# The receiver's linear term folded into the update's weights, and a table of normalised and raw rows for the edge gathers

## The reference, cut to what matters

```python
h = relu(layernorm(x))
m = concat([h[dst], h[src]]) @ W_pre.T + b_pre           # one message per edge
mx, mn, mean, std = segment max, min, mean, std of m over dst (0 for no edge; std = sqrt(relu(var) + 1e-5))
agg = concat([mx, mn, mean, std]);  log_deg = log(max(deg, 1) + 1)
out = concat([h, agg, agg*log_deg, agg/log_deg]) @ W_post.T + b_post
x = x + out @ W_lin.T + b_lin
h = relu(layernorm(x))
s = segment mean of edge_attr over dst
x = x + relu(concat([h, s]) @ W1 + b1) @ W2 + b2
```

## Time and profile before

| | |
|---|---|
| median of 3 runs | 1868.22 us (1868.07 to 1869.76) |
| profiled execution, span from first to last instruction | 1776.9 us |
| what lies around the span (difference of the two) | 91.3 us |
| busy in the span: PE / DVE / ACT / POOL | 86 / 89 / 60 / 73 % |
| HBM read and written | 98.3 MB and 38.8 MB |
| node pass, about | 40 to 540 us of the span |
| edge pass, about | 541 to 1777 us |

### The profile page before, as it was taken

How to read it: one execution, slowest core, us unless ns; L and a number is a source line. 1 busy time by engine, 2 the same in 40 slices (tenths; PEclk the granted TensorE clock), 3 DMA queues, 4 the chain that set the end, 5 groups by cost and what they waited for, 6 DMA issues and landing times.

```text
span 1776.9 us, 34948 instructions
## 1 busy us (share of the span) xinstructions
PE 1526.8 (86%) x8869; PEld 1275.2 (72%) x8869; DVE 1572.7 (89%) x5261; ACT 1067.4 (60%) x2368; POOL 1302.7 (73%) x1379
## 2 busy tenths in 40 slices
PE   2899999999997788888787879878787878888895
PEld 2799898998996577767675767667676667676774
DVE  5999999999996899989798979989797979899992
ACT  1899999999996455545454545545454545455541
POOL 1778777787787878877677777867786877778643
PEclk8899999999998899999999999989998999989997
DMA  2233333233325222222122221222122222222200
GB/s 75 83 101 106 95 105 104 97 106 99 102 95 142 61 68 69 69 63 63 54 71 70 70 68 52 73 70 73 48 73 71 75 70 69 66 60 75 70 18 17
DMA packets 104065, 134.10 MB, mean 75 GB/s; under 512 B 17344, under 2 KB 63577, under 8 KB 103978
## 3 DMA queue, kind: packets, MB, share of 16 engines
q1 hardware_dynamic: 85162, 98.55, 19.1%
q0 software_dynamic: 18816, 34.71, 6.7%
HBM read 98.27 MB, written 38.79 MB: 77 GB/s over the span
## 4 chain that ended last, share of the span: by engine, by line
DVE 42%; PE 36%; issue 17%; ACT 2%; POOL 1%; DMA 1%; DVEq 1%; SPq 0%; POOLq 0%; ACTq 0%
PE bank L556 10%; PE bank L565 5%; DVE runs L1204 3%; DVE runs L1189 3%; DVE part L1083 3%; DVE var L1240 3%; DVE var L1234 3%; DVE runs L1193 2%; PE bank L577 2%; PE bank L575 2%; DVE runs L1161 2%; PE bank L539 2%; PE bank L576 2%; DVE bn L1262 2%; PE bank L547 2%
## 5 line engine op out<-in xcount | busy, mean ns | idle before, releaser
L598 PE MATMUL bank<-comb_lo,agg_hi 128*128 128x384 f32 x588 | 221.7, 377 | 44.6 <-DVE nx L1092 36.5
L473 POOL DMA_INDIRECT y<-nout,oidx x196 | 212.2, 1083 | 54.6 <-issue 51.9
L460 POOL DMA_INDIRECT xs<-in_x,idx x196 | 203.1, 1036 | 65.0 <-issue 63.7
L460 POOL DMA_INDIRECT xd<-in_x,idx x196 | 185.5, 947 | 59.7 <-issue 59.4
L602 PE MATMUL bank<-comb_hi,agg_lo 128*128 128x384 f32 x588 | 209.6, 357 | 4.0 <-POOL agg_lo L400 4.0
L599 PE MATMUL bank<-comb_hi,agg_hi 128*128 128x384 f32 x588 | 209.0, 355 | 0.0
L556 PE MATMUL bank<-w_sb,nut 128*128 128x128 f32 x1568 | 203.8, 284 | 5.4 <-DVE nout L999 4.7
L377 POOL TENSOR_TENSOR runs<-nx,b_all 128x512 f32<-128x512 f32 x98 | 125.7, 1283 | 108.6 <-DVE nx L1009 107.6
L556 PEld LDWEIGHTS bank<-w_sb,nut 128*128 128x128 f32 x1568 | 185.6, 194 | 23.1 <-issue 14.2
L400 POOL TENSOR_TENSOR agg_lo<-whole,agg_hi 128x512 fp32r<-128x512 f32 x98 | 146.1, 1513 | 66.1 <-ACT agg_hi L848 66.1
L605 PE MATMUL bank<-comb_sd,agg_sd 128*128 128x384 f32 x392 | 169.9, 517 | 0.0
(11 more groups left out here) (196 smaller groups left out, 4788.3 us busy)
## 6 DMA issues: line engine op xcount, KB each, us to landing
xs<-in_x SPq DMA_DIRECT2D x98, 256.0 KB, 2.8
y<-nout SPq DMA_DIRECT2D x98, 256.0 KB, 2.8
inv<-inv_row SPq DMA_DIRECT2D x49, 256.0 KB, 4.6
attr<-in_edge_attr SPq DMA_DIRECT2D x48, 256.0 KB
keep<-keep_row SPq DMA_DIRECT2D x49, 128.0 KB, 2.7
reset<-reset_row SPq DMA_DIRECT2D x49, 128.0 KB, 3.1
lift<-lift_row SPq DMA_DIRECT2D x49, 128.0 KB, 4.0
xs<-in_x,idx POOLq DMA_INDIRECT x196
```

The costliest lines, as they stand in the source:

```text
L460: pool.indirect_dma_start(out=rows[:, s, j, :], out_offset=None, in_=x, in_offset=bass.IndirectOffsetOnAxis(ap=idx[:, s, which, j:j + 1], ...
L473: pool.indirect_dma_start(out=out, out_offset=bass.IndirectOffsetOnAxis(ap=oidx[:, c % 4, j:j + 1], axis=0), in_=eout[:, c % 2, j, :], in_ ...
L598: pe.matmul(acc[:, 0:SCALERS * P], hi, w_lo, start=(a == MX), stop=False, skip_group_check=True)
```

## The change

1. a is no longer computed. The aggregates are taken of b + b_pre, and a's share of max, min and mean goes into the weights of h[dst]: `comb_h` (three scalers, 384 wide) = Wd times the sums of the `comb` blocks of max, min and mean, plus `comb_x` for the first scaler. It is computed once at the start (9 + 4 more products on PE). This drops a's three matmuls and the three `whole` sums, and makes the last three products of each `layer0` 384 wide instead of 128. For nodes without an edge `comb_x` stays.
2. ACT copies b + b_pre from bank 3 to bank 4 (new, `e_b`), and the scans read bank 4; the square takes the bias too.
3. The node pass writes a table in HBM: for each node 256 floats, the normalised row (before the relu) and the raw row. The edges gather the normalised half for senders (512 B) and both halves for receivers (1 KB, one descriptor per row as before), so the edge pass has no first layernorm: eight statistics, eight aggregations and two small operations less on DVE, one square root and eight activations less on ACT.
4. The gathers wait until the whole table is stored. PE's transposes wait for the gathers directly.
5. The x rows of a node chunk now land with a row pitch of 1 KB in SBUF (512 B pieces), the load comes one step later (k+5) and waits for the table store of the chunk that had the slot.

```diff
+    table = nc.dram_tensor("table", [N, 2 * P], F32, kind="Internal").ap()
+    table_halves = table.rearrange("n (t f) -> (n t) f", t=2)
+    rows = sb("rows", [P, 4, TILES, 2 * P])
+    nh, nx = rows[:, :, :, 0:P], rows[:, :, :, P:2 * P]
+    hd, xd = nh, nx
...            SP, node_step
-                c = k + 6
+                c = k + 5
                 if node(c):
                     if c >= 4:
-                        sp.wait_ge(sem("n_norm1"), c - 3 + NU * i)
-                        sp.wait_ge(sem("n_norm1_act"), c - 3 + NU * i)
-                        sp.wait_ge(sem("n_norm1_pool"), c - 3 + NU * i)
+                        sp.wait_ge(sem(f"n_tabled{c % 4}"), 16 * (c // 4) + 16 * i)
+                        sp.wait_ge(sem("n_turn1"), c - 3 + NU * i)
                         sp.wait_ge(sem("n_xc"), c - 3 + NU * i)
                     sp.dma_start(nx[:, c % 4], node_rows(x, c, i)).then_inc(sem(f"n_in{c % 4}"), 16)
+                c = k + 2
+                if node(c):
+                    sp.wait_ge(sem("n_norm1"), c + 1 + NU * i)
+                    sp.wait_ge(sem("n_norm1_act"), c + 1 + NU * i)
+                    sp.wait_ge(sem("n_norm1_pool"), c + 1 + NU * i)
...
+                    sp.dma_start(node_rows(table, c, i), rows[:, c % 4]).then_inc(sem(f"n_tabled{c % 4}"), 16)
...            POOL, edge_step
                     if c == 0:
                         pool.wait_ge(sem("turned_out"), TURNS)
-                        pool.wait_ge(sem("n_norm1"), NODE_CHUNKS)
-                        pool.wait_ge(sem("n_norm1_act"), NODE_CHUNKS)
+                        for n in range(4):
+                            pool.wait_ge(sem(f"n_tabled{n}"), 16 * ((NODE_CHUNKS - n + 3) // 4))
+                        pool.wait_ge(sem("n_turn1"), NODE_CHUNKS)
...
-                        pool.wait_ge(sem("e_norm1"), c - 3 + EU * i)
-                        pool.wait_ge(sem("e_norm1d"), c - 3 + EU * i)
+                        pool.wait_ge(sem("e_turned_s"), c - 3 + EU * i)
+                        pool.wait_ge(sem("e_turned_d"), c - 3 + EU * i)
...
-                        for which, rows in ((0, xs), (1, xd)):
+                        for which, to, of in ((0, hs, table_halves), (1, rows, table)):
...            PE
+            for s in range(SCALERS):
+                for a in (MX, MN, ME):
+                    b = 1 + s * AGGS + a
+                    pe.matmul(bank[5][:, (1 + s) * P:(2 + s) * P], w_post_sb[:, b * P:(b + 1) * P], w_lin_t[:],
+                              start=(a == MX), stop=(a == ME))
...
-                for h, w in ((hdt, comb_x_lo), (hdl, comb_x_hi), (hdt, comb_x_hi)):
-                    mm = pe.matmul(acc[:, 0:P], h[:, c % 2, cols], w[:], start=False, stop=(w is comb_x_hi and h is hdt),
+                for h, w in ((hdt, comb_h_lo), (hdl, comb_h_hi), (hdt, comb_h_hi)):
+                    mm = pe.matmul(acc[:, 0:SCALERS * P], h[:, c % 2, cols], w[:].rearrange("p s f -> p (s f)"),
...            PE, edge_step
-                    pe.wait_ge(sem("e_norm1"), c + 1 + EU * i)
+                    pe.wait_ge(sem(f"e_gathered{c % 4}"), 16 * 2 * TILES * (c // 4 + 1) + 16 * 2 * TILES * i)
...
-                    pe.matmul(bank[4][:], wd_lo[:], hdt[:, c % 2, :], start=True, stop=False)
-                    pe.matmul(bank[4][:], wd_hi[:], hdt[:, c % 2, :], start=False, stop=False)
-                    pe.wait_ge(sem("e_hdl"), c + 1 + EU * i)
-                    pe.matmul(bank[4][:], wd_hi[:], hdl[:, c % 2, :], start=False, stop=True).then_inc(sem("e_a_psum"), 1)
...            ACT
+                    act.activation(bank[4][:], bank[3][:], ACT.Identity, bias=b_pre_col[:]).then_inc(sem("e_b"), 1)
...
-                    norm1(hs, xs, 0, sem("e_norm1"))
...
-                    norm1(hd, xd, TILES, sem("e_norm1d"))
...            DVE (the scans read bank 4; L1125, L1134, L1149, L1170, L1175 and L1253 go as well)
-                    dve.scalar_tensor_tensor(whole[:, MX, :], bank[4][:], b_pre_col[:], run_max[:, b, :],
-                                             ALU.add, ALU.add).then_inc(sem(f"e_whole{MX}"), 1)
```

More of the change, by code:

```diff
@@ L519, in _ @@
             mm.then_inc(sem("turned"), 1)
+            pe.wait_ge(sem("part_sum_ready"), 1)
+            for s in range(SCALERS):
+                to = bank[5][:, s * P:(s + 1) * P]
+                mm = pe.matmul(to, w_pre_sb[:, 0:P], part_sum[:, s, :], start=True, stop=(s > 0))
+                if s == 0:
+                    mm = pe.matmul(to, w_post_sb[:, 0:P], w_lin_t[:], start=False, stop=True)
+            mm.then_inc(sem("comb_h_psum"), 1)
             pe.wait_ge(sem("comb_copied"), 1)
@@ L538, in node_step @@
                     for j in range(TILES):
[L539 removed]
+                        mm = pe.transpose(bank[0][:, j * P:(j + 1) * P], nh[:, c % 4, j, :], ident[:])
                     mm.then_inc(sem("n_turn1"), 1)
@@ L812, in edge_step @@
                     act.wait_ge(sem("e_b_psum"), c + 1 + EU * i)
+                    if c >= 1:
+                        act.wait_ge(sem("e_sum"), c + EU * i)
+                    act.activation(bank[4][:], bank[3][:], ACT.Identity, bias=b_pre_col[:]).then_inc(sem("e_b"), 1)
                     if c >= 2:
                         act.wait_ge(sem("e_sqsum"), c - 1 + EU * i)
[L815 to L833 removed]
+                    act.activation(bsq[:, c % 2, :], bank[3][:], ACT.Square, bias=b_pre_col[:]).then_inc(sem("e_bsq"), 1)
                 c = k - 1
@@ L839, in edge_step, with high_part @@
                     act.activation(h2t[:, c % 2, :], bank[0][:], ACT.Relu).then_inc(sem("e_h2t"), 1)
-                if edge(k + 2):
-                    norm1(hd, xd, TILES, sem("e_norm1d"))
-                def high_part(a, rows):
+                def high_part(a, made, rows):
                     c = k + 1
-                    act.wait_ge(sem(f"e_whole{a}"), c + 1 + EU * i)
+                    act.wait_ge(sem(made), c + 1 + EU * i)
                     if c >= 2:
@@ L1120, in edge_step @@
                     dve.reciprocal(rs2[:, b, :], sd2[:, b, :]).then_inc(sem("e_rs2"), 1)
-                if edge(k + 2):
-                    b, s = k % 2, (k + 2) % 4
-                    for j in range(2):
-                        dve.bn_stats(bn1[:, b, TILES + j, :], xd[:, s, j, :])
                 if behind:
@@ L1130, in edge_step @@
                                              ALU.mult, ALU.mult).then_inc(sem("e_ms2"), 1)
-                if edge(k + 2):
-                    b, s = k % 2, (k + 2) % 4
-                    for j in range(2, TILES):
-                        last = dve.bn_stats(bn1[:, b, TILES + j, :], xd[:, s, j, :])
-                    last.then_inc(sem("e_bn1"), 1)
-                    dve.wait_ge(sem("e_bn1"), k + 3 + EU * i)
                 if ahead:
@@ L1143, in edge_step @@
                                              ALU.max, ALU.subtract).then_inc(sem("e_hdl"), 1)
-                elif edge(k + 2):
-                    dve.memset(stats_go[:], 0.0)
-                if edge(k + 2):
-                    b = k % 2
-                    for j in range(2 * TILES):
-                        last = dve.bn_aggr(mv1[:, b, j, :], bn1[:, b, j, :])
-                    last.then_inc(sem("e_mv1"), 1)
                 if have:
@@ L1247, in edge_step @@
                     mix_plain(k, 2, i)
-                if edge(k + 3):
-                    c, b, s = k + 3, (k + 3) % 2, (k + 3) % 4
-                    dve.wait_ge(sem(f"e_gathered{s}"), 16 * 2 * TILES * (c // 4 + 1) + 16 * 2 * TILES * i)
-                    for j in range(TILES):
-                        dve.bn_stats(bn1[:, b, j, :], xs[:, s, j, :])
                 if have:
```

154 lines of the change are left out of this document (49 added, 105 removed).

## The result

The kernel after took 1674.6 us (median of four, 1669.5 to 1676.5) beside 1868.7 us of before (four, 1868.1 to 1869.8): a ratio of 0.896, 95% interval 0.894 to 0.897. The forecast was 1777 in a range of 1748 to 1842.

A forecast was written before the change was run, and what follows sets the result against it. DVE was taken to bound the edge pass before, POOL after at 22.2 us a step: first gather 549.1, 82 to k=2, 43 steps 954.6, tail 100, span 1686, plus 91.3 around it, 1777 us, range 1748 to 1842.

The forecast's parts named there:

- With the 91.3 around it: Last line of the sum: 91.3 us outside the profiled span, added to a span of 1686 to give 1777 us.
- Setup: Before the node pass: additional PE products for the new weights delay everything after by 4.4 us, bounds +2 and +7.
- The table's store: Node pass: storing 512 KB per chunk takes 3.6 us, 2.0 fixed plus 1.6, with room enough on DMA.
- (b): Node pass: held by its slots as latencies rise; 1816 us at a store plus load of 13 us; chance 0.10.
- POOL's own step, 22.17 us: Edge pass: POOL's step without its wait, 23.29 - 1.12 us; the change removes nothing from it.
- rival (e): Edge pass: POOL gets faster if its operations miss DVE, steps of 21.5 us, -30, 1747 us; chance 0.08.
- The round's stall: Edge loop: DVE's 7.1 us stand once per round stays or shrinks, covered by about 11 us of slack; may vanish.
- Rival (a): Edge loop: DVE's stand once per round is exposed, wholly or in part, up to +61, 1795 to 1838 us; chance 0.11.
- (c): Edge pass: 1 KB rows cost two descriptors, up to 1.02 us more per receiver gather, +200, 1977 us; chance 0.07.
- (d): Edge pass: PE becomes the bound as its clock falls below 0.89; at 0.85 +47, 1824 us; chance 0.06.
- (f): Edge pass: no gain because a chain over several engines holds the step at 23 to 24 us, 1830 to 1870; chance 0.02.
- DVE is the bound: Edge pass of before: DVE, 88% busy, sets the pace, since PE and POOL wait for it; POOL has almost no slack.

## Why the prediction was wrong where it was, and right where it was

**"With the 91.3 around it"** was the step that failed, in the last line of the sum. I took the difference between the profiled span and the timed median for a cost outside the program, which both kernels would pay. It was inside the program: the timed executions ran a slower edge pass than the profiled one, by the trace of a second execution 81 us in the 43 steps and 9.5 in the stand at 566 us, less 3 elsewhere. The runs beside the result put 194 us on the change; in a session where before ran quick it was worth 109. My forecast of the gain, 91 us, was a sum for the quicker rhythm, and is 18 us off there.

**The span, 18 us too long**, term by term: first gather at 544.39, forecast 549.1 (-4.7). From there to k=2 83.4, forecast 82 (+1.4). The 43 steps 944.0, forecast 954.6 (-10.6). From there to the end 95.9, forecast 100 (-4.1).

**Setup** (+4.4 forecast) and hand-over (+3.2): the first gather was at 541.54 in before, so they cost 2.9 us together and not 7.6. The L379 ahead of the first gather starts at 540.68, where the old L377 started at 539.69: the setup costs 1.0. PE made the additional products, but began with them at 21.02 instead of 23.34, which the sum had not looked for. The other 1.9 are the hand-over, with 1.5 us in which POOL waits for the last table store. **The table's store** lands in 2.7 us, the page says:
```profile
table<-rows SPq DMA_DIRECT2D x98, 512.0 KB, 2.7
rows<-in_x SPq DMA_DIRECT2D x98, 256.0 KB, 3.1
```
I had 3.6 by doubling a transfer's share, and the Trainium skill's formula (DMA: Bandwidth & Descriptors, Anatomy of one DMA) gives 3.2; that section is about DMAs that GpSimd issues, and this one is issued by SyncE. Both are too high: twice the bytes cost nothing beside the 2.8 us of 256 KB. Node steps kept their pace, so (b) did not happen, as argued.

**POOL is the bound afterwards**: right, and shown by the three kernels with more work on POOL, on PE and on DVE together. **POOL's own step, 22.17 us**: 21.95 measured. The two low parts take 1.28 instead of 1.52 us each and the scatters 1.00 instead of 1.10, probably because they meet a DVE that is less busy; against that `gather_go` takes 0.6 instead of 0.2 and a receiver's gather 0.06 more. That is rival (e) in a small part; it had 21.5.

**The round's stall is hidden or gone**: right, and more than hidden. POOL's L413 comes every 21.1 to 22.3 us between 651 and 892 us, with no long step among them, and POOL waits for nobody to the end of the loop. The prediction named the Trainium skill's rule (Runtime: NRT & Kernel Launch, Instruction fetch mechanics), by which the stall might vanish with 21 of 56 DVE operations gone, and the trace agrees: the packets of instructions fell from 70 to 22, the page's queue rows say (before, then after):
```profile
q14 instruction: 70, 0.57, 0.1%
```
```profile
q14 instruction: 22, 0.18, 0.0%
```
The kernel with its edge loop written out adds that the unexplained stand at `nout` goes with the jump, worth 23 us there. Rival (a) fell.

**(c) POOL pays by bytes** fell by the gathers' rows. **(d) PE's clock** fell too: between 1100 and 1200 us it rose from 0.93 to 0.97. **(f)** fell: nothing but POOL holds the step.

**"DVE is the bound" of before** was half right. Within a round the profiled execution ran at 22.2 to 23.3 us, POOL's own pace or a little over; DVE's share was the long step per round. In the slower rhythm DVE was held in every step. "The waits name DVE" did not tell these apart, the list of POOL's starts did.

## What to carry to other kernels

Compare the profiled span with the timed executions before adding anything: in every other profiled execution here they were 1.8 to 2.1 us apart. If they differ by more, the profile may show another rhythm of the kernel than the one that is timed, and no sum from it reaches the timed one. A second profile of the same kernel, laid beside the first up to where they part, costs one run. One kernel, in which several engines hand work round in a ring, had two rhythms 5% apart; the one that POOL paces, with slack on DVE and ACT, ran at one speed in its two sessions. The way to test what paces a kernel is to give each engine a microsecond more, and to read the steps and not only the time: here 10 us of the time came and went in a single first step.

## What the runs showed that I had not expected

- Before: timed at 1857.7 to 1871 us in some sessions and 1764 to 1779 in others, on one and the same chip too (1859.8 and 1773.0). Its cause is open.
- In the slower rhythm, where it parts from the other, ACT gets on 2.5 us after the modelled end of the matmul it waits for; in 12 of 35 later steps the profile calls the releaser of this wait "remote". In the quicker one it gets on 0.04 us after. Whether the matmul itself ran later than modelled is open.
- Small DVE operations stretch beside a busy POOL: the same 128x4 product takes 531 ns on average in after, 1809 and 2114 in the two executions of before, and 3054 with the low part on DVE. The longest, in before, lasts until POOL's fourth operation in a row ends (L400 twice, L485, L413, 605.18 to 610.14 us):
```profile
605.09 5.08 DVE L1129 SCALAR_TENSOR_TENSOR ms<-mv,rs 128x4 f32<-128x4 f32 x1
```
- With 0.86 us more of PE work per step the granted clock in the edge pass was 1.00 instead of 0.97, and the time no longer; it was 1.00 as well with more statistics on DVE and with one low part moved, which give PE nothing more, and 0.94 with one more operation on POOL.
